# Lists for the routed experts' tiles: one list of forty made at the end, or a first list of nine made early and the rest later

## The chip, the core and the metric

The kernel runs on one core of one Trainium2 chip. The engines are PE (TensorE, matrix products), DVE (VectorE), ACT (ScalarE), POOL (GpSimd) and SP (SyncE, which here only issues DMAs). They run side by side and meet at semaphores. The metric is the device time of one execution in microseconds, lower is better.

## The reference, cut to what matters

A small vision network of five parts works on 8 x 257 = 2056 tokens of 256 values: a state-space tokenizer, an attention, a layer of routed experts, a second attention with a feed-forward part, and a quantised feed-forward. The change touches the routed experts alone:

```python
xf = x.reshape(-1, C)                       # 2056 x 256, normalised rows
gate_logits = xf @ Wr                       # 8 experts
w, idx = jax.lax.top_k(gate_logits, TOP_K)  # TOP_K = 2
w = jax.nn.softmax(w, axis=-1)
comb = jnp.sum(w[:, :, None] * jax.nn.one_hot(idx, NUM_EXPERTS, dtype=w.dtype), axis=1)
h = jnp.einsum('nc,ech->neh', xf, W1)       # hidden width 384
g = jnp.einsum('nc,ech->neh', xf, W3)
y = jnp.einsum('neh,ehc->nec', jax.nn.silu(h) * g, W2)
out = jnp.einsum('nec,ne->nc', y, comb)
```

## The kernel before, in words

The kernel is one program of stages, each a block in which every engine has its own instruction stream; a stage begins when all engines are through the one before. `routed_experts` (from L1022) is the third of six. It computes only what the routing asks for: each token's row goes to its two experts, and the experts' rows are worked off in tiles of 128.

**Tokens and groups.** The tokens lie in SBUF as 17 tiles of 128 rows (`TILES`; the last, `CLS`, has 8 rows: the class tokens). They are routed in five groups (`GROUPS`, L1083): tiles 0 to 1, 2 to 3, 4 to 7, 8 to 11, 12 to 16. For each group, PE turns the normalised rows and multiplies them with the gate's matrix (L1405, L1416); DVE's `choose(g)` (L1218 to L1239) finds the two largest of eight logits and writes `sel`, a one for each chosen expert; PE's `ranks(g)` (L1425, L1429) counts with triangular and all-one matrices how many rows of each expert stand before each token, in one PSUM bank (`RB` = 3); DVE's `place_rows(g)` (L1243 to L1260) turns the count into two row numbers for each token in the HBM buffer `x_rows`, where each expert has a region of 17 tiles (`REGION`), and raises `placed`. Behind the reading of the counts it raises `rank_read`.

**Scatters.** POOL (L1156 to L1163) writes the rows into `x_rows` with indirect DMAs, two for each token tile, 34 in all, one after the other, each group behind its `placed`. Those of the first eight token tiles (`FIRST_ROWS`) count on the semaphore `scattered_first`, the others on `scattered`.

**Expert tiles.** There is room for 40 (`NT`) expert tiles of 128 rows. The first nine (`FULL`) are taken from regions that the first eight token tiles alone fill to whole tiles of 128 (8 x 128 x 2 rows over 8 experts give at least nine of them). `full_tiles()` (L1264 to L1275), behind the third group's placing, counts them: `cum` is the running sum by expert, cut at nine, and `used` how many of the nine each expert gives. The other 31 take what is left, expert by expert.

**The list.** Behind `place_rows(4)`, DVE makes one list for all 40 tiles (L1296 to L1330): from `used` and the remaining number of tiles it forms running sums (`ends`) over 16 parts, compares each tile number with each of them (`past`, 40 x 16 = 640 elements in each partition), and derives from that the expert of each tile (`owner_i`) and the row in `x_rows` where it starts (`row_i`), by sums over the 16 parts. L1330 raises `owned`. Behind the list (L1332 to L1353) DVE computes where in the packed output each token's two rows will be (`packed`, `pos_i`) and (L1355 to L1370) the two weights of each token (`share`); both are read in the next stage. ACT's exponential for the weights (L1176) waits for the differences of L1297.

**The order of the stage's second half.** SP waits for `owned` (L1103). `load(t)` (L1106 to L1114) reads the row number of tile t from `row_i` into a register (L1107), for t = 0 waits for `scattered_first`, for t = 9 for `scattered`, from t = 4 on for a free buffer of four, and loads 128 rows of `x_rows` into `xin`. The first four loads come at once, then one in each turn of a loop that also stores results. PE waits for `owned` (L1441); then `turn_rows(t)` (L1443) transposes the loaded tile into banks 0 and 1, `up` (L1452) makes the two products with the expert's W1 and W3 (banks 2 to 5), `turn_hidden` (L1459) transposes the hidden rows, `down` (L1468) multiplies with W2. In the loop from L1479 PE's order for tile t is: transpose rows of t + 1, `up` 0 of t, transpose hidden of t - 1, `up` 1 of t, `down` of t - 1. ACT copies transposed rows (L1182), computes SiLU (L1196) and copies results (L1189). DVE's loop (L1386 to L1390) has only `turned(t - 1)` (copy of transposed hidden rows, L1383) and `hidden(t)` (SiLU times second product, L1377).

`s(...)` issues an instruction that counts on the engine's own semaphore; `s.wait()` waits for all that were issued before. Dependent steps are so separated by it.

## Time and profile before

| | |
|---|---|
| Median of three runs | 1336.87 us (1335.01 to 1336.89) |
| The profiled execution | 1331.12 us, its span 1329.4 us |
| Mean granted clock of PE in it | 0.865 of full speed |
| Busy over the span | PE 83%, DVE 59%, POOL 35%, ACT 29% |
| The routed experts' stage | from about 250 to 480 us |

The profile is one execution, recorded by the hardware; the durations below all come from it. Times in microseconds count from the start of its span. A timeline row gives start, length, engine, line and operation, what is written and read, and in brackets how long the engine had been idle and what ended that. Granted clock 1.00 is 2.4 GHz, 0.50 is 1.2 GHz.

### The profile page before, as it was taken

How to read it: one execution, taken by the hardware profiler on the slowest of the kernel's cores; microseconds unless marked ns; L12 is line 12 of the kernel's file. 1: busy time of each engine (PE TensorE's matmuls, PEld its weight loads, DVE VectorE, ACT ScalarE, POOL GpSimd, SP SyncE). 2: the span in 40 equal slices, each digit the busy share in tenths (PEclk: the TensorE clock that was granted, in tenths of full speed). 3: DMA queues.
4: the chain of work that ended last, by engine and by line, in shares of the span. 5: the costliest groups of instructions: out<-in, count | busy, mean ns of one | idle time of the engine just before them, and what ended most of it. 6: DMA issues, size and time to landing. Idle time of an engine off the chain costs nothing. (4 is left out here: it accounts for less than half of the span.)

```text
span 1329.4 us, 22071 instructions
## 1 busy us (share of the span) xinstructions
PE 1105.6 (83%) x6752; PEld 792.8 (60%) x6752; DVE 780.3 (59%) x1860; ACT 385.7 (29%) x951; POOL 467.3 (35%) x579
## 2 busy tenths in 40 slices
PE   0267898859999945799999999999889999689898
PEld 0166776556777722556656566565548998455555
DVE  8965666562222233667575575755733776588884
ACT  0242333102222211233343333432304443222221
POOL 4962000271000035122232222220115776376665
PEclk9978999659999977578696886967778999799999
DMA  9908000222111116155152461523214000000000
GB/s 318 307 1 285 1 0 0 72 103 77 61 60 60 60 33 115 48 94 110 48 109 73 79 114 39 109 76 48 83 35 137 0 0 0 1 9 8 16 16 17
DMA packets 66431, 93.81 MB, mean 71 GB/s; under 512 B 9152, under 2 KB 58760, under 8 KB 65200
## 3 DMA queue, kind: packets, MB, share of 16 engines
q1 hardware_dynamic: 63152, 84.42, 24.3%
q0 software_dynamic: 3200, 8.43, 2.0%
q8 instruction: 38, 0.62, 0.2%
q14 instruction: 41, 0.34, 0.1%
HBM read 52.23 MB, written 40.33 MB: 70 GB/s over the span
## 5 line engine op out<-in xcount | busy, mean ns | idle before, releaser
L2200 DVE TENSOR_REDUCE fa_nm<-fa_ps 128x2 f32<-128x514 f32 x128 | 83.0, 690 | 84.2 <-PE fa_ps L2442 83.5
L1455 PE MATMUL ex_ps<-we_raw,ex_xT 128*128 x320 | 117.5, 490 | 0.0
L1993 ACT ACTIVATE fa_eT<-fa_ps 128x512 f32<-128x512 f32 x128 | 73.6, 590 | 71.1 <-PE fa_ps L2495 69.7
L3243 PE MATMUL qf_ps<-qf_wg,qf_xT 128*128 128x352 f32 x272 | 90.0, 480 | 2.1 <-ACT qf_xT L3084 1.4
L2442 PE MATMUL fa_ps<-fa_ks,fa_qs 64*128 64x258 f32 x256 | 73.5, 419 | 21.6 <-DMA fa_ks<-fa_qk_rows 16.9
L451 PE MATMUL tk_ps<-tk_u,tk_qb 64*32 64x64 f32 x1024 | 24.8, 274 | 69.6 <-POOLq L318 56.7
L1383 DVE COPY ex_hT<-ex_ps 128x384 f32<-128x384 f32 x40 | 22.3, 559 | 100.1 <-PE ex_ps L1464 100.1
L2442 PEld LDWEIGHTS fa_ps<-fa_ks,fa_qs 64*128 64x128 f32 x256 | 52.7, 268 | 47.2 <-issue 30.7
L2495 PE MATMUL fa_ps<-fa_qs,fa_ks 66*128 66x256 f32 x256 | 71.1, 372 | 7.0 <-ACT fa_eT L1993 7.0
L3243 PEld LDWEIGHTS qf_ps<-qf_wg,qf_xT 128*128 128x128 f32 x272 | 50.7, 195 | 37.3 <-issue 6.8
L1455 PEld LDWEIGHTS ex_ps<-we_raw,ex_xT 128*128 128x128 f32 x320 | 55.4, 193 | 22.1 <-issue 1.1
L2874 PE MATMUL ff_ps<-ff_xT,wg_f 128*128 128x128 f32 x544 | 65.9, 282 | 3.2 <-ACT ff_xT L2773 3.2
L2874 PEld LDWEIGHTS ff_ps<-ff_xT,wg_f 128*128 128x128 f32 x544 | 65.7, 198 | 4.3 <-issue 3.5
L3231 PE MATMUL qf_ps<-qf_wd,qf_hT 128*128 128x256 f32 x204 | 53.2, 404 | 17.5 <-DVEq L3152 12.0
L2888 PE MATMUL ff_ps<-wg_f,ff_hid 128*128 128x256 f32 x272 | 63.1, 386 | 2.8 <-DVEq L2814 2.8
L451 PEld LDWEIGHTS tk_ps<-tk_u,tk_qb 64*32 64x32 f32 x1024 | 22.9, 146 | 71.3 <-issue 71.3
L2495 PEld LDWEIGHTS fa_ps<-fa_qs,fa_ks 66*128 66x128 f32 x256 | 43.9, 209 | 34.3 <-issue 20.0
L1765 POOL DMA_INDIRECT fa_xn<-y_rows,pos_i x2 | 1.8, 878 | 175.9 <-POOLq L1098 175.6
L1473 PE MATMUL ex_ps<-we_raw,ex_hT 128*128 x240 | 58.4, 379 | 0.7 <-DVE ex_hT L1383 0.7
L2888 PEld LDWEIGHTS ff_ps<-wg_f,ff_hid 128*128 128x128 f32 x272 | 51.4, 194 | 9.7 <-issue 3.2
L3231 PEld LDWEIGHTS qf_ps<-qf_wd,qf_hT 128*128 128x128 f32 x204 | 36.9, 194 | 31.2 <-ACT qf_hT L3095 21.3
L2780 ACT ACTIVATE ff_hid<-ff_ps,wg_c 128x128 f32<-128x128 f32 x136 | 37.0, 383 | 61.7 <-PE ff_ps L2874 61.7
(487 smaller groups left out, 2487.8 us busy)
## 6 DMA issues: line engine op xcount, KB each, us to landing
x_rows<-tk_zero SPq DMA_DIRECT2D x8, 2176.0 KB, 17.5
we_raw<-in_L_ffn_W SPq DMA_DIRECT2D x24, 384.0 KB, 7.3
fa_qs<-fa_qk_rows SPq DMA_DIRECT2D x16, 514.0 KB, 8.7
fa_ks<-fa_qk_rows SPq DMA_DIRECT2D x32, 257.0 KB, 10.7
ex_xin<-x_rows SPq DMA_DIRECT2D x40, 128.0 KB, 2.0
y_rows<-ex_y SPq DMA_DIRECT2D x40, 128.0 KB, 1.7
fa_rsb<-fa_rs_rows SPq DMA_DIRECT2D x32, 132.0 KB, 2.8
fa_qk_rows<-fa_qhl SPq DMA_DIRECT2D x32, 128.5 KB
```

The source lines that it names most:

```text
L451: last = nc.tensor.matmul(ps[outs, p, i * n:(i + 1) * n], QB[rows, p, r, j * HB // 2 + i, :], U[rows, p, r, j * HB // 2 + i, :], start=(r ...
L1455: last = mm(ps[:, bank + t % 2, 0:HD], xT[:, t % 2, k, :], raw[:, ds(e, 1), m, k * HD:(k + 1) * HD], start=(k == 0), stop=(k == KC - 1))
L1473: last = mm(ps[:, YB, 0:SEQ], hT[:, t % 2, j, :], raw[:, ds(e, 1), 2, j * SEQ:(j + 1) * SEQ], start=(j == 0), stop=(j == NJ - 1))
L1993: cp(eT[:, j % 8, :], ps[:, ST + j % 2, :], ACT.Exp).then_inc(z["e_ready"], 1)
L2200: nc.vector.tensor_reduce(nm[:, :, j], ps[:, b:b + 2, 0:TOK], AX.X, ALU.max, negate=True).then_inc(z["max_done"], 1)
L2442: last = mm(ps[:, b + t, 0:WID], qs[0:ROWS, p, head(j, 1 + t * P, P)], ks[0:ROWS, p, head(j, 0, WID)], start=True, stop=True)
L2495: last = mm(ps[:, ST + j % 2, c * SEQ:(c + 1) * SEQ], ks[0:ROWS + 2, p, head(j, 1 + c * P, P)], qs[0:ROWS + 2, p, head(j, 1, SEQ)], start= ...
L2780: nc.scalar.activation(hid[:, p, f, :], ps[:, HB + 2 * p + f // 4, (f % 4) * P:(f % 4 + 1) * P], ACT.Relu, bias=w["c1"][:, f:f + 1]).then_ ...
L2874: last = mm(ps[:, HB + 2 * p + f // 4, (f % 4) * P:(f % 4 + 1) * P], w["f1"][:, k, f * P:(f + 1) * P], xT[:, p, k, :], start=(k == 0), sto ...
L2888: last = mm(ps[:, YB + p, 0:SEQ], hid[:, p, f, :], w["f2"][:, f, :], start=(f == 0), stop=(f == NF - 1))
L3231: last = mm(ps[:, YB, 0:SEQ], hT[0:n, c, :], wd[0:n, c, :], start=(c == 0), stop=(c == NH6 - 1))
L3243: last = mm(ps[:, GB + 2 * g + a, 0:HALF], xT[:, k, :], wg[:, g, k, a * HALF:(a + 1) * HALF], start=(k == 0), stop=(k == KC - 1))
```

## The change

DVE's one list becomes two. `first_list()` makes owners and rows of tiles 0 to 8 and runs behind `choose(3)`, ahead of `place_rows(3)`; it uses `cum` directly (8 parts for 9 tiles: 72 elements). The list of the other 31 tiles (8 parts, 248 elements) is cut in three: `other_parts()` stands behind `place_rows(4)`, `other_owners()` behind the hidden product of tile 0, `other_rows()` behind that of tile 1. `packing()`, `positions()`, `weights()` and the two `shares()` stand behind those of tiles 2 to 6. The differences for the weights move ahead of `place_rows(4)`. `owned` is now raised twice: SP and PE wait for the first at their start, and for the second at tile 9 (`FULL`). PE gets a wait for the fifth `rank_read` ahead of the first `turn_rows`, since the counts' bank and the logits' banks are used again. Three memsets and one wait of POOL at the stage's start go. The numbers that come out are the same.

```diff
@@ experts, SP @@
             def load(t):
+                if t == FULL:
+                    sp.wait_ge(z["owned"], 2)
                 rows[t] = nc.sync.value_load(row_i[0:1, t:t + 1], min_val=0, max_val=(ROW_TILES - 1) * P)
                 if t == 0:
                     sp.wait_ge(z["scattered_first"], 16 * 2 * FIRST_ROWS)
@@ experts, POOL @@
-            s(g.memset(next_owner[:, :], 1.0))
             s(g.memset(cum[:, 0:1], 0.0))
-            s(g.memset(off[:, 2 * NE:2 * NE + 1], float(ROW_TILES - 1)))
-            s.wait()
-            s(g.memset(next_owner[:, NE - 1:NE], float(1 - NE)))
-            s(g.memset(next_owner[:, 2 * NE - 1:2 * NE], 0.0))
+            s(g.memset(off[:, :, NE:NE + 1], float(ROW_TILES - 1)))
             s.wait()
@@ experts, DVE, place_rows @@
                 if hi == FIRST_ROWS:
                     s(ts(full_i[:, :], rank[:, hi, :], 0.0, None, ALU.add))
+                if hi == TILES:
+                    s(ts(cnti[:, :], rank[:, hi, :], float(P - 1), None, ALU.add))
                 s.wait()
                 dve.sem_inc(z["rank_read"], 1)
@@ experts, DVE @@
+            FIRST, REST = slice(0, FULL), slice(FULL, NT)
+
+            def first_list():
+                s(tt(past[:, FIRST, :], bc(nth[:, FIRST], 2, NE), bc(cum[:, 1:NE + 1], 1, FULL), ALU.is_ge))
+                s(tt(off[:, 0, 0:NE], region[:, :], cum[:, 0:NE], ALU.subtract))
+                s.wait()
+                s(nc.vector.tensor_reduce(owner[:, FIRST], past[:, FIRST, :], AX.X, ALU.add))
+                s(tt(step[:, 0, :], off[:, 0, 1:NE + 1], off[:, 0, 0:NE], ALU.subtract))
+                s.wait()
+                s(tt(behind[:, FIRST, :], past[:, FIRST, :], bc(step[:, 0, :], 1, FULL), ALU.mult))
+                s(ts(owner_i[:, FIRST], owner[:, FIRST], float(NE - 1), None, ALU.min))
+                s.wait()
+                s(nc.vector.tensor_reduce(begin[:, FIRST], behind[:, FIRST, :], AX.X, ALU.add))
+                s.wait()
+                s(tt(begin[:, FIRST], nth[:, FIRST], begin[:, FIRST], ALU.add))
+                s.wait()
+                s(ts(row_i[:, FIRST], begin[:, FIRST], float(ROW_TILES - 1), float(P), ALU.min, ALU.mult))
+                s.wait()
+                dve.sem_inc(z["owned"], 1)
+
+            def other_parts():
+                s(ts(cnti[:, :], cnti[:, :], 7, None, ALU.logical_shift_right))
+                s.wait()
+                s(nc.vector.tensor_copy(cnt[:, :], cnti[:, :]))
+                s.wait()
+                s(tt(parts[:, :], cnt[:, :], used[:, :], ALU.subtract))
+                s.wait()
+                s(nc.vector.tensor_tensor_scan(ends[:, :], ones[:, 0:NE], parts[:, :], 0.0, ALU.mult, ALU.add))
+                s.wait()
+                s(tt(past[:, REST, :], bc(nth[:, 0:NT - FULL], 2, NE), bc(ends[:, :], 1, NT - FULL), ALU.is_ge))
+                s(tt(start[:, :], ends[:, :], parts[:, :], ALU.subtract))
+                s.wait()
+                s(tt(ahead[:, :], used[:, :], start[:, :], ALU.subtract))
+                s.wait()
+
+            def other_owners():
+                s(nc.vector.tensor_reduce(owner[:, REST], past[:, REST, :], AX.X, ALU.add))
+                s(tt(off[:, 1, 0:NE], region[:, :], ahead[:, :], ALU.add))
+                s.wait()
+                s(ts(owner_i[:, REST], owner[:, REST], float(NE - 1), None, ALU.min))
+                s(tt(step[:, 1, :], off[:, 1, 1:NE + 1], off[:, 1, 0:NE], ALU.subtract))
+                s.wait()
+                s(tt(behind[:, REST, :], past[:, REST, :], bc(step[:, 1, :], 1, NT - FULL), ALU.mult))
+                s.wait()
+
+            def other_rows():
+                s(nc.vector.tensor_reduce(begin[:, REST], behind[:, REST, :], AX.X, ALU.add))
+                s.wait()
+                s(stt(begin[:, REST], nth[:, 0:NT - FULL], off[:, 1, 0:1], begin[:, REST], ALU.add, ALU.add))
+                s.wait()
+                s(ts(row_i[:, REST], begin[:, REST], float(ROW_TILES - 1), float(P), ALU.min, ALU.mult))
+                s.wait()
+                dve.sem_inc(z["owned"], 1)
...
             choose(3)
+            first_list()
             place_rows(3)
             choose(4)
+            differences()
             place_rows(4)
-
-            s(ts(cnti[:, :], rank[:, TILES, :], float(P - 1), None, ALU.add))
-            s(tt(wt[:, :, :], lg[:, :, 0:NE], top[:, :, 0:1].broadcast_to([P, TILES, NE]), ALU.subtract))
...
-            s(tt(past[:, :, :], bc(nth[:, :], 2, 2 * NE), bc(ends[:, :, :].rearrange("p a e -> p (a e)"), 1, NT), ALU.is_ge))
...
-            s(tt(behind[:, :, :], past[:, :, :], bc(next_owner[:, :], 1, NT), ALU.mult))
...
-            dve.sem_inc(z["owned"], 1)
...
+            other_parts()
...
                 hidden(t)
+                if t == 0:
+                    other_owners()
+                elif t == 1:
+                    other_rows()
+                elif t == 2:
+                    packing()
+                elif t == 3:
+                    positions()
+                elif t == 4:
+                    weights()
+                elif t == 5:
+                    shares(0)
+                elif t == 6:
+                    shares(1)
             turned(NT - 1)
@@ experts, PE @@
             owners = [None] * NT
+            pe.wait_ge(z["rank_read"], len(GROUPS))
             turn_rows(0)
             for t in range(NT):
+                if t == FULL:
+                    pe.wait_ge(z["owned"], 2)
                 owners[t] = nc.tensor.value_load(owner_i[0:1, t:t + 1], min_val=0, max_val=NE - 1)
```

`packing()`, `positions()`, `weights()` and `shares(a)` hold the old L1332 to L1346, L1348 to L1353, L1355 to L1363 and one turn of L1364 to L1370, with `jump` formed from `ahead` and `cum` in one operation.

## Rows read from the trace of the kernel before

**Rows 1.** Windows of core 0, busy us of each engine in two stretches
```profile
core 0: us, PE busy (x) PEld busy (x) DVE busy (x) ACT busy (x) POOL busy (x), PEclk, DMA share, GB/s
256.00:294.00 38.00, 27.31 (x129) 26.91 (x127) 22.87 (x132) 4.08 (x8) 24.53 (x24) 0.50 0.29 108
294.00:300.00 6.00, 1.11 (x4) 0.75 (x5) 5.30 (x24) 1.43 (x2) 4.48 (x6) 0.50 0.46 151
```

**Rows 2.** Timeline of PE, 284 to 304 us: start, length, idle before and releaser
```profile
284.02 2.28 PE L1429 MATMUL ex_ps<-ex_sel,ex_ones 128*128 128x40 f32 x10
297.85 0.66 PE L1448 MATMUL ex_ps<-ident,ex_xin 128*128 128x128 f32 x2 [11.55 <-DMA ex_xin<-x_rows]
299.55 0.69 PE L1448 MATMUL ex_ps<-ident,ex_xin 128*128 128x128 f32 x2 [1.03 <-DMA ex_xin<-x_rows]
300.03 3.90 PE L1455 MATMUL ex_ps<-we_raw,ex_xT 128*128 x8
```

**Rows 3.** Waits of SP's own queue, 255 to 330 us
```profile
SPq L1107 <- DVEq L1330: 37.2, 1, 37.2
```

**Rows 4.** Timeline of SP's queue, first loads and that of tile 9
```profile
295.67 5.51 SPq L1114 DMA_DIRECT2D ex_xin<-x_rows  x5
...
327.64 0.33 SPq L1114 DMA_DIRECT2D ex_xin<-x_rows  x1
```

**Rows 5.** Instructions that read ex_row_i: shortest, median, longest ns; first start
```profile
L1107 SPq TENSOR_LOAD <-ex_row_i x40: 262/269/531, 294.7 to 459.6; - x40
```

**Rows 6.** Timeline of DVE, 275 to 297 us
```profile
275.56 0.19 DVE L1237 TENSOR_TENSOR ex_sel<-ex_lr,ex_valid 128x32 f32<-128x32 f32 x1
278.27 0.19 DVE L1246 TENSOR_TENSOR ex_place<-ex_ps,ex_base 128x32 f32<-128x32 f32 x1 [2.52 <-PE ex_ps L1429]
...
286.34 0.20 DVE L1246 TENSOR_TENSOR ex_place<-ex_ps,ex_base 128x40 f32<-128x40 f32 x1 [2.88 <-PE ex_ps L1429]
286.69 0.20 DVE L1251 TENSOR_TENSOR ex_place<-ex_place,ex_sel 128x40 f32<-128x40 f32 x1
...
289.31 0.82 DVE L1310 TENSOR_TENSOR ex_past<-ex_nth,ex_ends 128x640 f32<-128x640 f32 x1
...
291.26 0.81 DVE L1317 TENSOR_REDUCE ex_owner<-ex_behind 128x40 f32<-128x640 f32 x1
...
294.36 0.23 DVE L1328 TENSOR_SCALAR ex_row_i<-ex_begin 128x40 int32<-128x40 f32 x1
294.74 0.17 DVE L1332 SCALAR_TENSOR_TENSOR ex_delta<-ex_start,ex_base 128x8 f32<-128x8 f32 x1 [0.15 <-DVE ex_row_i L1328]
...
296.91 0.30 DVE L1348 TENSOR_REDUCE ex_pos<-ex_packed 128x17 f32<-128x136 f32 x1
```

**Rows 7.** Timeline of POOL: the sixteenth scatter, a stretched one, the last
```profile
281.73 0.96 POOL L1160 DMA_INDIRECT x_rows<-ex_xn,ex_into  x1 [0.30 <-issue]
...
289.36 1.59 POOL L1160 DMA_INDIRECT x_rows<-ex_xn,ex_into  x1 [0.30 <-issue]
...
305.79 0.85 POOL L1160 DMA_INDIRECT x_rows<-ex_xn,ex_into  x1 [0.31 <-issue]
```

**Rows 8.** Line L1160 (scatters): time from issue to landing
```profile
DMA to landing us min/median/max: 2.0/2.4/3.2
```

**Rows 9.** Timeline of DVE in the first expert tiles
```profile
304.02 0.55 DVE L1377 TENSOR_TENSOR ex_hid<-ex_sl,ex_ps 128x384 f32<-128x384 f32 x1 [3.02 <-PE ex_ps L1455]
305.80 0.56 DVE L1383 COPY ex_hT<-ex_ps 128x384 f32<-128x384 f32 x1 [1.22 <-PE ex_ps L1464]
...
310.23 0.56 DVE L1383 COPY ex_hT<-ex_ps 128x384 f32<-128x384 f32 x1 [2.58 <-PE ex_ps L1464]
```

**Rows 10.** Timeline of PE in the first expert tiles
```profile
306.89 1.46 PE L1473 MATMUL ex_ps<-we_raw,ex_hT 128*128 x6
...
311.32 1.46 PE L1473 MATMUL ex_ps<-we_raw,ex_hT 128*128 x6
```

**Rows 11.** Windows of core 0, the microsecond with the clock's rise (columns as above)
```profile
302.00:303.00 1.00, 1.00 (x4) 0.67 (x3) 0.00 (x0) 0.33 (x1) 0.93 (x1) 0.83 0.73 250
```

133 lines of the change are left out of this document (55 added, 78 removed).

## The prediction

> **What bounds the kernel now.** I read the windows first, by stretch of the experts' stage. From 256 to 294 us PE works on gate logits and ranks for 27.3 of 38 us; from 294 to 300 it is busy for 1.11 of 6 us while DVE is busy for 5.30 [rows 1]. From the first expert product on, the PE timeline has no idle time until the stage's last tile. So the stage is bound by PE as soon as the first tile runs, and the stretch before that by something else. The page's chain of waits does not reach this stretch, so I follow the hand-over with the timelines. On PE, the last rank product ends at 286.30 and the first transposition of gathered rows starts at 297.85: 11.55 us idle, put down to the load of ex_xin [rows 2]. On SP's own queue, the read of the first row number waited 37.2 us for DVE's semaphore of L1330; it starts at 294.7, and the first load at 295.67 [rows 3 to 5]. On DVE, the last placing starts at 286.34, and the list of the 40 tiles' owners and rows ends with L1328, which starts at 294.36 [rows 6]. So the first load is late because of one chain of small operations on DVE; its data, the first eight tiles' scattered rows, had landed long before (next part). Whatever brings that load forward brings the whole PE-bound stage forward.
>
> **The first list, moved.** It has six dependent steps, four of them on 9 x 8 = 72 elements (three have a second, independent operation beside). The 128x40 operation takes 0.20 us and the 128x136 one 0.30 [rows 6], so 72 elements take about 0.23; with 0.03 to 0.04 between dependent ones and some 0.1 for each second operation the list is about 1.8 us. It starts where L1237 of the fourth group ends, 275.75, and ends at about 277.6. The next DVE instruction waits for PE until 278.27, an idle time of 2.52 us [rows 6]: that is the cover, and the cost is nothing. If it took 1 us more, only the fourth group's scatters would wait, and POOL reaches those behind the sixteenth, at 283.0 (281.73 and 1.26 more [rows 7]).
>
> **What holds the first load next.** SP reads the first row number at 277.7 and then waits for the 16 scatters of the first eight tiles. POOL issues them one after the other, 1.26 us apart; the sixteenth starts at 281.73 and lands 2.0 to 3.2 us later, median 2.4 [rows 7, 8]: 284.13, bounds 283.73 and 284.93. The row number is read by then. Behind its read, of 0.53 us at most, the old load started at 295.67, 0.44 after 295.23 [rows 4, 5]: that is the upper bound from release to load, nothing the lower one, and I take the middle, 0.2 us. So the first load starts at 284.33 instead of 295.67: **11.34 us earlier**, between 11.94 and 10.30.
>
> **What else could hold PE.** PE's new wait is for the fifth reading of the ranks. L1251 starts at 286.69, behind that reading [rows 6]; the change puts one more 128x8 operation ahead of it, 0.08 us: 286.8. Behind this wait stands all of PE's work for tile 0, but the load lands at 284.33 + 2.18 = 286.5 (297.85 less 295.67), so the first transposition starts at 286.8 and ends at 287.5. The second tile's load is what counts before the first product: it came 3.88 us after the first load's start (299.55 less 295.67), and the product 4.36 after it (300.03) [rows 2, 4]. In the new kernel that is 288.2 and 288.7. Both are past 287.5, so the wait for the ranks costs nothing; it would count only if it ended past 287.5. The load of old competed with a busier DMA, so up to 0.5 us more could be gained; I leave it out. **Term: 11.3 us.**
>
> **The rest of the list** (other_parts): seven operations of 8 elements and one of 31 x 8 = 248. From 136 elements in 0.30 and 640 in 0.81 [rows 6], 248 take 0.42. About 1.8 us from 287.8 to 289.6; DVE's first product comes at 304.02 - 11.3 = 292.7. Hidden; the cover has 3 us to spare. The old list had five operations of 640 elements, 4.1 us in all; the new one has four of 248 and four of 72.
>
> **The parts dealt out among the tiles.** Each stands behind hidden(t) and ahead of turned(t). In the first gap DVE idles 1.22 us, later 2.58 us [rows 9]. turned(0) ends at 306.36 and PE's next product that needs it starts at 306.89; for tile 1 these are 310.79 and 311.32 [rows 9, 10]: so 0.53 us of slack more. The pieces: other_owners two of 248 and small ones, 0.54 + 0.30 + 0.46 = 1.3 us against 1.22 + 0.53; other_rows 1.0; packing, from L1332 at 294.74 to L1348 at 296.91, 2.17 [rows 6]; positions 1.0, weights 1.3 and each share 1.0, by their steps of 136 elements at 0.30 and 0.03 between (positions two, side by side, and two short ones; weights four; a share three); these against 2.58 + 0.53 = 3.11. All fit. If the cover were gone, their 8.8 us would come onto the path. The tightest are the first, with 0.45 us to spare, and packing, with 0.94.
>
> **Waits of tile 9.** The old kernel issues the load of tile 9 (counted from 0) at 327.64 [rows 4]; the new one at 316.3. The last scatter starts at 305.79 [rows 7] and lands at 308.2, or 309.0 at the most; the second part of the list is ready behind hidden(1), 296.3 + 1.0. Both new and old waits find their semaphores up, with 7 us of margin. Differences before the last placing: 0.3 us in an idle stretch of 2.88 [rows 6]; memsets taken from POOL at the start of the stage: nothing waits for them. Nothing behind this stage is changed, so it should all move forward by the same amount.
>
> **Sum.** 11.3 us off the profiled execution's 1331.12 us gives 1319.8. The median of the runs shown is 1336.87, which is 5.75 above that execution; the same 11.3 us there gives **1325.6 us**.
>
> **A rule against the change.** While POOL scattered, DVE's operations kept their times: the 640-element L1310, with a scatter beside it, took 0.82 us and L1317 0.81. But that scatter, begun 0.05 us after L1310, took 1.59 us instead of 0.96 [rows 6, 7]. So a DVE operation with two inputs delays a scatter by about its own rest; 72-element ones ahead of the sixteenth scatter cost at most 0.1 each, 0.2 in all, within the bounds. The Trainium skill, "SBUF — State Buffer", in its part on ports and contention, says that VectorE and GpSimd share a port pair as an exclusive lock: whichever starts first holds it for its whole instruction, also against a VectorE operation with two SBUF inputs. By that rule the DVE pieces could be the blocked side too, which no row here shows.
>
> **The rivals.**
> (a) *DVE's pieces are held by scatters.* Scatters run until 306, so the pieces behind tiles 0, 1 and 2 (292.7 to 303) share the time with them. If each piece were held once for a whole scatter of 0.96: other_owners 2.3 against 1.75, packing 3.1 against 3.1; held twice, packing is 1 us late. That is 0.5 to 3 us for three pieces: gain 8.3 to 10.8, 1328.6 to 1326.1 us. Against it: the even DVE times above.
> (b) *PE's clock, the side that is slower.* The granted clock was 0.50 up to 300 and 0.83 in the mean of 302 to 303 [rows 1, 11]: with 0.50 before the rise and 1.00 behind it, PE went from 1.2 to 2.4 GHz at about 302.3. It had worked without gaps since 299.55. Eight products took 3.90 us over it [rows 2], some 0.64 us apart before and 0.33 behind it, so a tile at 1.2 GHz costs 4.4 us more than the 4.43 us that it takes (311.32 less 306.89 [rows 10]). The new start has the same order of work and the same gaps, so the rise should come at the same distance, within a microsecond either way, worth 0.5. But if small gaps from a late DVE piece kept the clock down for two tiles, 8.8 us are given back: 1334.4, no change. From 2.6 tiles on the kernel is slower; with three it gains 11.3 - 13.3 = -2.0, with four -6.4: 1338.9 to 1343.3 us. The page "TensorE: Matmul & The Clock Gate" of the Trainium skill says, in its part on the clock gate, that the activity window runs freely and the number of slow matmuls varies from run to run; by that the half microsecond is luck. Against (b): the work up to 294 kept PE at 0.50 though it was nearly always busy, so no earned clock is lost by the change.
> (c) *The hole only moves.* If the first load went on waiting for something of DVE's last group, or tile 9 stalled on the scatters, what is gained at 297 is lost at 316. The code excludes the first (the semaphore is raised behind L1237's group, before the last placing); the second needs scatters 7 us late, where the stretched one of old was 0.63 late (1.59 less 0.96). Full loss gives 1336.9, no change. That the change doesn't do what it says is this rival too.
> (d) *More than the forecast.* The second load lands 0.5 us sooner and the clock rises up to 2 us sooner: gain 12.8, 1324.1 us, or 1323 with the landing at its minimum.
>
> **How the numbers follow.** Forecast 0.80; (a) 0.07; (b) 0.04, half of it no change and half slower; (c) 0.02; (d) 0.07. The range: gain 12.8 plus 0.5 for the landing, and about 1.5 us of scatter between medians (the three runs shown lie within 1.9 us) gives the low end, 1322; the high end takes in the bounds (10.3), a late clock (0.5), most of (a) and the same scatter: a gain of 5.9, 1331. A change of 0.2% is 2.7 us, about what a measurement of this kernel can tell from none. Faster 0.94, no change 0.04, slower 0.02.
>
> **What would show it.** First ex_xin load at 284.3 (wrong if past 285.5); first transposition at 286.8, released by the ranks rather than by the load; first product at 288.7; DVE's small operations between its tile operations with PE's products without gaps from there; PE's tile rhythm 4.43 us; load of tile 9 at about 316; the stage's last product ends at 467.6 instead of 478.9. Wrong would be: gaps on PE behind DVE ex_hT in tiles 0 to 6, a granted clock of 0.50 beyond 292, or PE waiting at tile 9.

## The result and the profile after

| | before | after |
|---|---|---|
| median of 20 executions each (us) | 1338.69 (1333.48 to 1347.76) | 1333.24 (1326.50 to 1338.30) |
| ratio after to before, 95% interval | | 0.9949 (0.9935 to 0.9963) |
| profiled execution (us) | 1331.12 | 1337.93 |
| its span (us) | 1329.4 | 1336.2 |

The change makes the kernel faster by 5.45 us, where 11.3 us were forecast, and the time, 1333.24 us, is above the range of 1322 to 1331. Put beside each other, the two profiled executions say the opposite, 6.8 us slower. The execution of before that was profiled was shorter than each of the 20 executions behind the median of before. That turns out to be part of the explanation, so each distance below is given with the execution it is from. By the ratio's interval the gain lies between 5.0 and 8.7 us. Of the 6.8 us between the two profiled executions, 3.0 stand at the stage's last product (219.28 us behind the first scatter against 216.24) and 3.8 come in the stages behind it.

The windows of the changed kernel (columns as in [rows 1]):

```profile
core 0: us, PE busy (x) PEld busy (x) DVE busy (x) ACT busy (x) POOL busy (x), PEclk, DMA share, GB/s
256.00:300.00 44.00, 29.53 (x135) 28.32 (x134) 20.09 (x131) 5.67 (x10) 24.29 (x25) 0.50 0.31 112
300.00:314.00 14.00, 10.98 (x39) 6.54 (x38) 4.48 (x15) 2.35 (x8) 8.46 (x9) 0.92 0.19 77
314.00:345.00 31.00, 30.89 (x132) 21.63 (x133) 13.10 (x38) 8.34 (x23) 0.00 (x0) 1.00 0.21 65
```

From 256 to 300 us PE is busy for 29.5 us, hardly more than in the two rows of [rows 1] together (28.4), although the load of gathered rows was to come 11 us earlier. From 314 us on PE is full at clock 1.00; from 300 to 314 it misses 3 us.

The timeline of PE, changed kernel (start, length, line, idle before it and releaser; as in [rows 2, 10]):

```profile
291.55 0.65 PE L1469 MATMUL ex_ps<-ex_sel,ex_before 128*128 128x40 f32 x2 [8.92 <-DVEq L1238]
292.00 2.28 PE L1473 MATMUL ex_ps<-ex_sel,ex_ones 128*128 128x40 f32 x10
297.70 0.66 PE L1492 MATMUL ex_ps<-ident,ex_xin 128*128 128x128 f32 x2 [3.42 <-issue]
...
299.05 4.37 PE L1499 MATMUL ex_ps<-we_raw,ex_xT 128*128 x8
...
309.53 1.46 PE L1499 MATMUL ex_ps<-we_raw,ex_xT 128*128 x4
314.11 1.56 PE L1517 MATMUL ex_ps<-we_raw,ex_hT 128*128 x6 [3.13 <-DVE ex_hT L1413]
...
318.64 1.46 PE L1517 MATMUL ex_ps<-we_raw,ex_hT 128*128 x6
...
323.06 1.46 PE L1517 MATMUL ex_ps<-we_raw,ex_hT 128*128 x6
```

The first transposition of gathered rows (L1492) starts at 297.70, almost where it was (297.85 [rows 2]) and not at 286.8. Two holes stand ahead of it: 8.92 us ahead of the fifth group's rank products (L1469), and 3.42 us ahead of the transposition, with no DMA as the releaser. A third, of 3.13 us, follows at tile 1 (314.11). From 318.64 on the rhythm is 4.42 us a tile.

SP's queue and the first of the reads of the row numbers, changed kernel ([rows 4, 5] before; the second fence is the view of line L1110):

```profile
285.79 13.08 SPq L1117 DMA_DIRECT2D ex_xin<-x_rows  x5
```

```profile
L1110 SPq TENSOR_LOAD <-ex_row_i x40: 3/269/700, 279.1 to 462.7; - x40
```

The row number was read at 279.1 and the first load went out at 285.79, 9.88 us earlier than at 295.67 [rows 4]. So the part of the change that its name speaks of did happen. But the five loads of this group took 13.08 us in place of 5.51. The fifth waits for a free buffer; the first four have no wait between them in the code, and they start at 285.79, 288.61, 295.68 and 297.23, over 11.44 us where the kernel before needs 3.88 (295.67 to 299.55).

The timeline of DVE, changed kernel ([rows 6, 9] before):

```profile
277.33 0.23 DVE L1279 TENSOR_TENSOR ex_past<-ex_nth,ex_cum 128x72 f32<-128x72 f32 x1
...
278.84 0.23 DVE L1292 TENSOR_SCALAR ex_row_i<-ex_begin 128x9 int32<-128x9 f32 x1
...
286.55 0.20 DVE L1220 COPY ex_lg<-ex_ps 128x40 f32<-128x40 f32 x1 [5.60 <-remote]
...
288.67 0.20 DVE L1232 TENSOR_TENSOR ex_lr<-ex_lr,ex_lg 128x40 f32<-128x40 f32 x1 [0.37 <-DVE ex_lr L1229]
290.07 0.20 DVE L1236 TENSOR_TENSOR ex_sel<-ex_lr,ex_valid 128x40 f32<-128x40 f32 x1 [1.20 <-DVE ex_lr L1232]
...
297.27 0.20 DVE L1245 TENSOR_TENSOR ex_place<-ex_ps,ex_base 128x40 f32<-128x40 f32 x1 [5.38 <-remote]
...
299.60 0.42 DVE L1305 TENSOR_TENSOR ex_past<-ex_nth,ex_ends 128x248 f32<-128x248 f32 x1
...
303.52 0.55 DVE L1407 TENSOR_TENSOR ex_hid<-ex_sl,ex_ps 128x384 f32<-128x384 f32 x1 [3.23 <-PE ex_ps L1499]
...
309.47 0.18 DVE L1326 TENSOR_SCALAR ex_row_i<-ex_begin 128x31 int32<-128x31 f32 x1
313.41 0.56 DVE L1413 COPY ex_hT<-ex_ps 128x384 f32<-128x384 f32 x1 [3.76 <-remote]
```

The last placing (L1245) starts at 297.27; before it started at 286.34 [rows 6]. PE had ended its rank products at 294.28 (292.00 + 2.28), so DVE saw them 3 us late. The choice of the fifth group (L1220, 286.55) was 3.9 us late: PE's gate logits had ended at 282.64. Even between two operations of DVE itself, L1232 and L1236, stand 1.20 us where the same pair of the third group, at 268.15 and 268.38, has 0.04. At tile 1, PE's transposition L1508 ended at 309.69 and DVE took it up at 313.41. The word "remote" is the profile's for a release that it can't place at any instruction of this moment. ACT shows the same at the same time, its first store of ex_y waiting 7.52 us:

```profile
313.26 0.38 ACT L1188 ACTIVATE ex_y<-ex_ps 128x256 f32<-128x256 f32 x1 [7.52 <-remote]
```

What runs beside all this is POOL with its scatters:

```profile
261.12 1.25 POOL L1159 DMA_INDIRECT x_rows<-ex_xn,ex_into  x1 [7.58 <-DVEq L1261]
...
270.27 0.98 POOL L1159 DMA_INDIRECT x_rows<-ex_xn,ex_into  x1 [0.30 <-issue]
274.36 0.95 POOL L1159 DMA_INDIRECT x_rows<-ex_xn,ex_into  x1 [3.10 <-DVEq L1261]
...
293.29 0.96 POOL L1159 DMA_INDIRECT x_rows<-ex_xn,ex_into  x1 [0.30 <-issue]
298.96 0.96 POOL L1159 DMA_INDIRECT x_rows<-ex_xn,ex_into  x1 [4.70 <-DVEq L1261]
...
310.26 0.85 POOL L1159 DMA_INDIRECT x_rows<-ex_xn,ex_into  x1 [0.31 <-issue]
```

They come in three trains, that is rows of scatters with no more than 0.31 us of idle time between two, one scatter each 1.26 us (1.31 in the first): 8 of them up to 271, 16 from 274.36 to 294.25 and 10 from 298.96 to 311.1. The late hand-overs lie in the trains and end 2 to 3 us behind them: 297.27 behind 294.25, 313.3 behind 311.1.

### The profile page after: what moved, and what is told of

The parts are those of the page before. It is cut to its first block and busy times, and to the rows that moved or that the text cites. A ratio compares the mean times of both kernels' runs of the same rounds, so it can differ in the third digit from the quotient of the medians.

```text
span 1336.2 us, 22077 instructions
## 1 busy us (share of the span) xinstructions
PE 1107.7 (83%) x6752; PEld 794.3 (59%) x6752; DVE 777.3 (58%) x1867; ACT 385.0 (29%) x951; POOL 465.6 (35%) x576
## 5 line engine op out<-in xcount | busy, mean ns | idle before, releaser
L2489 PEld LDWEIGHTS fa_ps<-fa_ks,fa_qs 64*128 64x128 f32 x256 | 53.5, 273 | 45.4 <-issue 29.5
L1413 DVE COPY ex_hT<-ex_ps 128x384 f32<-128x384 f32 x40 | 22.3, 558 | 95.3 <-PE ex_ps L1508 91.5
L1517 PEld LDWEIGHTS ex_ps<-we_raw,ex_hT 128*128 128x128 f32 x240 | 45.3, 190 | 19.1 <-issue 5.4
```

The lines of the kernel that those rows point to most:

```text
L1517: last = mm(ps[:, YB, 0:SEQ], hT[:, t % 2, j, :], raw[:, ds(e, 1), 2, j * SEQ:(j + 1) * SEQ], start=(j == 0), stop=(j == NJ - 1))
L2489: last = mm(ps[:, b + t, 0:WID], qs[0:ROWS, p, head(j, 1 + t * P, P)], ks[0:ROWS, p, head(j, 0, WID)], start=True, stop=True)
```

## The experiments

All times below are from profiles where not said otherwise. So that executions can be laid over each other, events are counted from the start of the first scatter of the same execution. "Placing" is the last placing on DVE, "load" the first load of gathered rows, "first" the first transposition of them on PE and "end" the last expert product; each is a start. `scatter_late` is not in the table, since its first scatter comes only behind its last placing.

| run | placing | load | first | end |
|---|---|---|---|---|
| before, the profile shown ahead | 25.20 | 34.53 | 36.71 | 216.24 |
| before_a | 35.79 | 45.04 | 47.24 | 228.17 |
| before_b | 35.74 | 45.00 | 47.26 | 226.72 |
| before_2 | 35.74 | 45.00 | 47.26 | 226.69 |
| after | 36.15 | 24.67 | 36.58 | 219.28 |
| again | 36.18 | 24.73 | 36.62 | 219.31 |
| change_2 | 35.81 | 24.58 | 36.24 | 218.81 |
| first_only | 36.17 | 24.70 | 36.61 | 222.29 |
| deal_only | 36.05 | 40.51 | 42.59 | 223.58 |
| held | 36.16 | 37.79 | 39.83 | 225.78 |
| paced | 36.25 | 25.64 | 36.68 | 219.66 |
| paced_before | 36.18 | 45.49 | 47.65 | 228.45 |
| half | 25.14 | 17.96 | 25.57 | 204.37 |
| half_before | 25.19 | 34.44 | 36.66 | 217.02 |
| break_once | 29.77 | 24.71 | 30.19 | 226.98 |
| breaks | 29.79 | 24.70 | 30.22 | 209.33 |
| breaks_2 | 29.57 | 24.58 | 30.01 | 210.01 |
| breaks_before | 25.19 | 34.43 | 36.59 | 217.80 |
| breaks_before_2 | 27.44 | 36.68 | 38.82 | 219.98 |

**The change again, and taken apart.** `again` is the changed kernel unaltered. `first_only` keeps the early list and has all the other pieces in one block; `deal_only` keeps the dealing and makes the first list late; `held` lets the early load wait for the last placing.

```diff
 # first_only
             other_parts()
+            other_owners()
+            other_rows()
+            packing()
+            positions()
+            weights()
+            shares(0)
+            shares(1)
...
-                if t == 0:
-                    other_owners()
...
 # deal_only
             choose(3)
-            first_list()
             place_rows(3)
...
             place_rows(4)
+            first_list()
             other_parts()
 # held
                 if t == 0:
+                    sp.wait_ge(z["placed"], len(GROUPS))
                     sp.wait_ge(z["scattered_first"], 16 * 2 * FIRST_ROWS)
```

> The changed kernel once more, to see whether its delays stand at the same places. In its first profile the first load started at 285.79 us, as forecast but for 1.45 us, and then engines waited 1 to 5 us for signals that had long been raised (DVE 5.60 and 5.38 us before L1220 and L1245, ACT 7.52 and DVE 3.76 us at tile 1). Theory A, the early loads bring this about: the same delays come again between 283 and 315 us, first product past 296 us, ratio to the kernel before 0.995. Theory B, a disturbance that falls anywhere and hit this profile: the delays are elsewhere or smaller, first product at 288.7 to 291, stage about 11 us ahead of the kernel before.

> The first list moved as in the change, but nothing dealt out: all the rest stands in one block behind the last placing (10.6 us from 287.8 to 298.4). If nothing disturbs, the first product of DVE is 5.5 us late and the gain is 5.8 us, ratio 0.9957. Theory A (delays belong to loads and scatters side by side): the delays stand here too, in the same stretch, and the gain is near nothing or the same as the full change's. Theory C (delays come from the pieces among the tiles): no delays, gain 5.8 us.

> Pieces dealt out as in the change, but the first list made behind the last placing, so that the first load starts at about 290.7 us instead of 295.7. Undisturbed gain 5.0 us, ratio 0.9963. Theory A: loads beside scatters again for 10 us, so delays as in the change. Theory C (delays come from the pieces): delays at tiles 0 to 2 as in the change (3.8 us at tile 1). Theory B: none or anywhere.

> The changed kernel, but SP's first load also waits for the last placing (287.8 us): first load 288.0, 3.7 us later than it could be, first product at 292.4. Undisturbed the gain is 7.6 us, ratio 0.9943. Theory A in its narrow form (loads during the last group's choice and ranks slow DVE's and PE's signals): no delays before 288 us and the kernel is as fast as the change or faster. Theory D (a long wait on a register-loaded load or on the scatters' semaphore by SP slows the signals of others): delays between 279 and 288 as before.

Measured, on one chip with 29 executions of before at 1340.83 us: again 1330.34 us, ratio 0.9927 (0.9902 to 0.9952); first_only 1333.83, 0.9953 (0.9929 to 0.9976); deal_only 1335.06, 0.9952 (0.9933 to 0.9971); held 1332.67, 0.9946 (0.9923 to 0.9969). All four are faster than before, and the intervals of the four ratios overlap, so the totals hardly tell them apart. The rows do. `again` repeats the profile of after to a tenth: the placing at 36.2 and the start of PE at 36.6 are no accident of one execution. `held` puts the load 13.1 us later and loses only 3.2 at the first transposition, so in the changed kernel PE is not waiting for the load: its wait for the fifth reading of the ranks is the one that ends last. In `held` and `deal_only` the first load goes out only behind the last placing, and the placing is as late (36.16 and 36.05), so the early loads don't bring the delay about. At the last product `first_only` is 3.0 us later than `again`, `deal_only` 4.3 and `held` 6.5. In `held`, 3.2 of these stand at the first transposition; the rest is mostly the clock: behind its hole of 3.14 us at tile 1 the granted clock is 0.50 (in the mean of 313 to 318 us), where `again` keeps 1.00 behind one of 2.99. What the block costs stands in the timeline of PE, first_only:

```profile
308.26 0.90 PE L1501 MATMUL ex_ps<-ident,ex_hid 128*128 128x128 f32 x3 [4.64 <-issue]
```

DVE is busy with the block and PE waits 4.64 us for the first hidden rows. Of the 8.8 us that the prediction set for the pieces without cover, 4.64 show as this hole. Behind it the granted clock is 0.50 up to 311 us and 0.82 in the mean of 311 to 312; some 3 us of work at half the clock cost 1.6 more. Against that, first_only has none of the hole of some 3 us that the changed kernel has at tile 1 (2.99 in `again`). The sum, 3.2, is near the 3.0 measured at the last product.

**Before, profiled twice more, and the scatters moved.** Is the late placing made by the change, and is it made by the scatters? `before_a` and `before_b` are the kernel before, unaltered. `scatter_late` is the changed kernel with all scatters behind the last placing.

```diff
             clear_spent(pool, mem)
 
+            pool.wait_ge(z["placed"], len(GROUPS))
             for t in range(TILES):
```

> The kernel before, profiled again. All four traces of changed kernels have the same delays between PE's and DVE's hand-overs from 270 to 297 us (DVE's L1245 of the third group 1.5 us late, the last choice 4 to 6 us late, the last placing 9.4 to 11 us late), also the one whose work up to 286 us is that of the kernel before. Theory E, the first profile of the kernel before was an unusually quiet execution: then the same delays stand here, its last placing at 296 to 297.5 us, its first load at 305 to 307, its span at 1338 to 1343. Theory F, the changed kernels bring the delays: last placing at 286.3 again, span near 1330.

> The same again, as a second draw. Theory E: last placing at 296 to 297.5 us; theory F: 286.3.

> The changed kernel, but POOL begins its scatters only behind the last placing, so that none runs beside the choosing and ranking. If the scatters (or their landings) delay the hand-overs between PE and DVE, then DVE's last placing starts at about 286.5 us without the scatters; if the delays have another source, it stands at 296 to 297.5 as before. The first load then waits for 16 scatters from about 288 (297.5) us, 20 us, so the kernel is slower: first product near 313 us (quiet) or 323, total 1337 to 1345 either way.

Measured, one execution each: 1344.63, 1339.40 and 1360.94 us, beside one of before at 1340.72. The timelines of DVE, PE and POOL of before_a:

```profile
296.86 0.20 DVE L1246 TENSOR_TENSOR ex_place<-ex_ps,ex_base 128x40 f32<-128x40 f32 x1 [11.19 <-remote]
```

```profile
286.23 2.28 PE L1429 MATMUL ex_ps<-ex_sel,ex_ones 128*128 128x40 f32 x10
308.31 0.66 PE L1448 MATMUL ex_ps<-ident,ex_xin 128*128 128x128 f32 x2 [19.80 <-DMA ex_xin<-x_rows]
```

```profile
293.23 0.96 POOL L1160 DMA_INDIRECT x_rows<-ex_xn,ex_into  x1 [0.31 <-issue]
298.47 1.02 POOL L1160 DMA_INDIRECT x_rows<-ex_xn,ex_into  x1 [4.28 <-DVEq L1260]
```

The kernel before has the same fault. Its PE ended the rank products at 288.51, and DVE took them up at 296.86: 8.35 us late, 2.7 us behind the end of the train at 294.19. In the profile that stands ahead of the prediction DVE idles 2.88 us there [rows 6]; here it idles 11.19. So PE starts its tiles at 47.24 behind the first scatter, not at 36.71. Both executions, and later a third (before_2), agree within 0.05 us on that. Of the four profiles of this kernel, the one on which the prediction rests is the exception.

The timeline of DVE in scatter_late, and the last scatter in that of POOL:

```profile
284.87 0.20 DVE L1246 TENSOR_TENSOR ex_place<-ex_ps,ex_base 128x40 f32<-128x40 f32 x1 [2.43 <-PE ex_ps L1474]
...
334.31 0.56 DVE L1414 COPY ex_hT<-ex_ps 128x384 f32<-128x384 f32 x1 [13.74 <-remote]
```

```profile
328.64 0.85 POOL L1160 DMA_INDIRECT x_rows<-ex_xn,ex_into  x1 [0.31 <-issue]
```

With no scatter beside them the ranks run as in the quiet profile: the last placing starts at 284.87 after 2.43 us of idle time. Then one train of 34 scatters runs from 286.59 to 329.5, and the late hand-overs go with it. DVE takes up the transposed hidden rows of tile 0 at 334.31, 13.2 us behind their end on PE at 321.11, and the release is again "remote". The delays follow the scatters, not the place in the code and not the change. They also cost more here than was expected: 1360.94 us against a forecast of 1337 to 1345.

**How many scatters are open.** One explanation was the number of scatters under way at a time. `paced` and `paced_before` let POOL wait, before the scatters of token tile t, until those of tile t - 2 have landed (semaphores split by parity), in the changed kernel and in the old one.

```diff
             for t in range(TILES):
                 n = rows_of(t)
+                if t >= 2:
+                    u = t - 2
+                    name, lo = ("scattered_first%d", 0) if u < FIRST_ROWS else ("scattered%d", FIRST_ROWS)
+                    pool.wait_ge(z[name % (u % 2)], 16 * 2 * ((u - lo) // 2 + 1))
```

`half` and `half_before` issue only one of the two scatters of each token tile, in either kernel. Half of the expert rows then keep what was there, so their results are not the reference's; the rest of the work is the same.

```diff
-                    sp.wait_ge(z["scattered_first"], 16 * 2 * FIRST_ROWS)
+                    sp.wait_ge(z["scattered_first"], 16 * FIRST_ROWS)
...
-                for a in range(2):
+                for a in range(1):
```

> The changed kernel, with POOL holding back the scatters of a token tile until those of the tile two before have landed (so at most four under way; undisturbed a scatter lands 2.4 us after its start and the next two take 2.5, so the hold costs nothing). Theory G1, the hand-overs are late because completions of scatters pile up: few under way, no pile, last placing near 286.5 us, first product at 288.7, ratio to the kernel before 0.985. Theory G2, it is the rate of one scatter every 1.26 us for more than 10 us that does it, not how many are open: delays as in the change, scatters either unchanged or later, ratio 0.994 or worse.

> The same holding back on the kernel before. G1: last placing at 286.3, first load at 295.7 as in its first, quiet profile, ratio 0.994 to the kernel before; the paced change is then faster than this by the 11.3 us of the forecast. G2: last placing at 295 to 297 us, ratio 1.000 or worse.

> The changed kernel with only one of a token's two scatters (half of the expert rows stay at what they were, the rest of the work is the same), so the train is 17 long instead of 34, at the same rate. If the delay grows with the length of the unbroken train, the eight scatters behind the third placing (10 us) delay DVE's hand-overs by 0 to 1.5 us, last placing at 286.5 to 288.5 and first load near 281 to 284, no delay at tile 1. If any scatter beside the hand-over delays it, the delays stay at 4 us and more.

> The kernel before with only one of a token's two scatters, to be set against the changed kernel with the same cut, where no hand-over was late (last placing 283.79 us, first transposition 284.22, stage ahead by 23 us). If the change is worth what the forecast said once no hand-over is late, this one has its first transposition at 295.3 us and takes 10.5 to 12 us more than the changed one cut in the same way: 1327 to 1329 us. If dealing out or the early list costs something by itself, the difference is under 8 us.

Measured: paced 1333.70 us, 0.9954 (0.9934 to 0.9973); paced_before 1341.78, 1.0004 (0.9988 to 1.0020), both beside a before of 1340.17; half 1316.74 in one execution, half_before 1325.18 in one. The pacing does nothing: placing at 36.25 and 36.18, as without it. At most four scatters can be open in it, and the distance between them stayed at 1.26 us. That excludes more than four open scatters as the cause, and no more: a scatter lands 2.0 to 3.2 us after its start in the profile of before [rows 8], so at 1.26 us apart hardly more than three are open anyway, and the added wait never held POOL (0.31 us idle at most inside the trains). Leaving half of them out removes the late hand-overs, in one execution of each kernel, on chips where before ran at 1340. The timelines of DVE, PE and POOL of half:

```profile
283.79 0.20 DVE L1245 TENSOR_TENSOR ex_place<-ex_ps,ex_base 128x40 f32<-128x40 f32 x1 [2.43 <-PE ex_ps L1473]
```

```profile
281.03 0.65 PE L1469 MATMUL ex_ps<-ex_sel,ex_before 128*128 128x40 f32 x2 [2.53 <-DVEq L1238]
281.48 2.28 PE L1473 MATMUL ex_ps<-ex_sel,ex_ones 128*128 128x40 f32 x10
284.22 0.66 PE L1492 MATMUL ex_ps<-ident,ex_xin 128*128 128x128 f32 x2 [0.47 <-issue]
```

```profile
274.00 0.96 POOL L1159 DMA_INDIRECT x_rows<-ex_xn,ex_into  x1 [0.30 <-issue]
277.42 0.96 POOL L1159 DMA_INDIRECT x_rows<-ex_xn,ex_into  x1 [2.46 <-DVEq L1261]
```

The placing is back at 25.14 with its 2.43 us of idle time, and the first transposition starts 0.47 us behind the rank products, as the prediction had it. (The first load goes out at 276.61, earlier than expected, since it waits for eight scatters only.) POOL's scatters now come in trains of four at most (five at the end), with 1.8 us or more between them. This pair also gives the price of the change without late hand-overs: 36.66 less 25.57 is **11.1 us** at the first transposition (11.3 forecast, from an old start at 36.71), 12.65 us at the last product and 8.4 us in the time of the two executions, which were not made on the same chip; `half_before` was expected to take 10.5 to 12 us more. The last product gains 1.56 us more than the first transposition, and most of it is the clock: from the second transposition to the rise of the granted clock `half` needs 2.7 us (0.60 in the mean of 287 to 288) and `half_before` 4.9 (0.71 in that of 303 to 304), and 2.2 us longer at half the clock cost 1.1. In the other direction, the stages behind the last product took 6.2 us longer in `half`.

**Breaking the train.** If it is the unbroken train that matters, the same 34 scatters with breaks should do. `break_once` holds the last 18 of them until the last placing is done. `breaks` adds five more breaks, each by a wait of POOL for PE's down projection of an early tile.

```diff
+    BREAKS = {11: 1, 12: 2, 13: 3, 14: 4, 15: 5}
...
                 pool.wait_ge(z["placed"], 1 + sum(t >= hi for _, hi in GROUPS))
+                if t == FIRST_ROWS:
+                    pool.wait_ge(z["placed"], len(GROUPS))
+                if t in BREAKS:
+                    pool.wait_ge(z["y_ps"], BREAKS[t])
```

(`break_once` has the first of the two conditions alone.)

> The changed kernel, but POOL stops behind its sixteenth scatter until the last placing is done, so that the last choice and ranks have no scatters beside them; the other 18 then run in one train beside the first expert tiles. Theory G2 (an unbroken train of more than some 10 us delays the hand-overs): last placing near 287 us, first product near 290, but then tiles 1 to 4 stall for up to 10 us until the train ends at about 312 us; total between 1325 and 1336. If only the choice and ranks suffer: 1321.

> As the last, and the 18 later scatters are also broken up: six at once, then the next token tiles behind the finished products of expert tiles 0 to 4 (two scatters each, four at the end). Theory G2: neither the ranks nor the tiles stall, last scatter lands at about 322 us, just in time for tile 9; first product at 289 to 290, no gap on PE behind it, total 1320 to 1323, ratio 0.985 to 0.988. If the breaks are too short to matter: 1328 to 1334 as the change.

Measured, beside a before of 1339.76 us: break_once 1339.86 us, 0.9993 (0.9976 to 1.0010); breaks **1322.95 us, 0.9866 (0.9839 to 0.9892)**. The timelines of PE in break_once, and of PE and POOL in breaks:

```profile
317.26 2.92 PE L1519 MATMUL ex_ps<-we_raw,ex_hT 128*128 x6 [14.31 <-DVE ex_hT L1415]
```

```profile
288.20 0.65 PE L1474 MATMUL ex_ps<-ex_sel,ex_before 128*128 128x40 f32 x2 [5.49 <-DVEq L1243]
...
291.39 0.66 PE L1497 MATMUL ex_ps<-ident,ex_xin 128*128 128x128 f32 x2 [0.47 <-issue]
```

```profile
283.27 0.96 POOL L1164 DMA_INDIRECT x_rows<-ex_xn,ex_into  x1 [0.30 <-issue]
293.16 0.96 POOL L1164 DMA_INDIRECT x_rows<-ex_xn,ex_into  x1 [8.93 <-DVEq L1266]
...
299.48 0.96 POOL L1164 DMA_INDIRECT x_rows<-ex_xn,ex_into  x1 [0.30 <-issue]
302.55 0.96 POOL L1164 DMA_INDIRECT x_rows<-ex_xn,ex_into  x1 [2.11 <-PE ex_ps L1522]
```

In break_once the placing comes at 29.77 instead of 36.2 and PE starts 6.4 us earlier, but all of it is lost again, and 7.7 us more at the last product (the median, 1339.86, lies above the 1325 to 1336 expected): the remaining 18 scatters form one train, from 290.91 to 313.2, and PE stands still for 14.31 us at tile 1, until 4 us behind it. With breaks, the last 18 come as six, four times two and four, with 1.8 to 2.2 us of idle time on POOL between them; PE has no such hole, and the last product comes 10 us earlier than in the changed kernel (209.33 against 219.31). What is left is in the first 16 scatters: behind the train of eight, 274.42 to 284.2, PE still waits 5.49 us for DVE's choice (2.53 in half).

**The breaks without the change, and all side by side.** `breaks_before` and `breaks_before_2` put the same breaks into the kernel before; `breaks_2`, `change_2` and `before_2` repeat breaks, after and before.

> The kernel before with the same breaks among the scatters as in the last kernel, so that in neither a hand-over is much delayed; the two differ by the change alone. If the forecast's sum holds for such a kernel, the first transposition stands about 38 us behind the first scatter (25.2 to 27.1 for the last placing, 9.3 for the list, 2.2 for the load), 9 to 11.3 us behind that of the changed kernel with breaks, the ratio to the kernel before is 0.993 to 0.996 and 0.992 for changed against unchanged. If the breaks alone gave the 17 us, it is at 0.987 to 0.989 too.

> The changed kernel with breaks among the scatters. Where hand-overs are late without breaks: first transposition 30.2 us behind the first scatter, no stall behind it, ratio 0.986 to 0.988. Where they are not late (a quiet chip or time): as the changed kernel alone within 1 us.

> The kernel before with breaks. Where hand-overs are late without them: 4 to 7 us faster than the kernel before (ratio 0.995 to 0.997), and 8 to 11 us slower than the changed kernel with breaks. In a quiet time: ratio 1.000.

> The changed kernel once more, side by side with the next three on one chip, since in the last run the kernel before itself took 1329.8 us instead of 1340: there the delays may be missing on a chip or for a time. Forecast of the sum: first transposition 10 to 11.3 us ahead of the kernel before where no hand-over is late (then ratio 0.992, and 11.3 us), 10.7 where both are late (47.3 less 36.6 us behind the first scatter), of which tile 1's stall takes 3 back: ratio 0.993 to 0.995.

> The kernel before, for its profile next to those three. Late hand-overs: last placing 35.7 us behind the first scatter and span near 1338. Quiet: 25.2 us and span near 1329.

Measured, the first alone: breaks_before 1329.72 us beside a before of 1329.77 on the same chip, 1.0005 (0.9985 to 1.0025). The profile of breaks_before has no late hand-over (placing at 25.19), and before itself, of which no profile was taken on that chip, was 10 us below its other medians; so most likely that chip, or that hour, had none at all, and the ratio says that breaks neither help nor hurt a kernel whose hand-overs are on time. It says nothing on the cause. The changed kernel did not run there: what the change is worth where nothing is late is shown by the pair half and half_before alone.

The other four ran together on another chip, with 23 executions of before at 1339.81 us:

| | median us | ratio to before (95%) | first | end |
|---|---|---|---|---|
| before_2 (one execution) | 1341.69 | | 47.26 | 226.69 |
| change_2 | 1331.57 | 0.9952 (0.9928 to 0.9977) | 36.24 | 218.81 |
| breaks_before_2 | 1333.75 | 0.9961 (0.9938 to 0.9984) | 38.82 | 219.98 |
| breaks_2 | 1325.36 | 0.9900 (0.9869 to 0.9931) | 30.01 | 210.01 |

PE's first transposition, in breaks_2 and in breaks_before_2:

```profile
290.76 0.66 PE L1497 MATMUL ex_ps<-ident,ex_xin 128*128 128x128 f32 x2 [0.47 <-issue]
```

```profile
298.37 0.66 PE L1453 MATMUL ex_ps<-ident,ex_xin 128*128 128x128 f32 x2 [11.42 <-DMA ex_xin<-x_rows]
```

Change and breaks add up, though breaks_2 at 0.990 stays short of the 0.986 to 0.988 expected. Either alone takes 6 to 8 us off the 1339.81, both take 14.5. On the broken trains the change is worth 8.8 us at the first transposition (38.82 less 30.01), 10.0 at the last product and 8.4 in the medians; on the unbroken ones 11.0, 7.9 and 8.2.

**What else goes with the delays.** The profiles show three more things that bear on the cause. First, each scatter raises its semaphore 16 times when its rows have landed, and a trace has a record of each raise: 544 for 34 scatters. In the two profiles with 34 scatters and no late hand-over (before, breaks_before) all 544 are there. In the sixteen others there are only 106 to 266, and in half and half_before, which have no late hand-over, 126 and 177 of 272. The profile gives a time to landing only where none is missing, as its lists of issues show, in before and in before_a:

```profile
x_rows<-ex_xn,ex_into POOLq DMA_INDIRECT x34, 2.4
```

```profile
x_rows<-ex_xn,ex_into POOLq DMA_INDIRECT x34
```

Second, it is not only the hand-overs that are slow. SP's MOVE before each load only sets a register and waits for no other engine; here are its shortest, median and longest time in ns, in before and in after:

```profile
L1114 SPq MOVE ex_xin<-x_rows x40: 29/29/38, 295.6 to 460.3; - x40
```

```profile
L1117 SPq MOVE ex_xin<-x_rows x40: 29/29/701, 285.7 to 463.3; - x40
```

Third, the engine that waits is not the late part: the record of PE's raise for the last placing stands at 297.24 in after and at 296.83 in before_a, and DVE starts 0.03 us behind it. PE's products had ended at 294.28 and 288.51 by the profile, which models the ends of products.

So there is a rival that no run tests: the recording itself. Either the train of scatters slows the engines and the recording suffers with them, or writing so many records is what slows the engines. The executions that are listed one by one, also behind the medians, all have a recorded span and clock; none is known to show the kernel unrecorded. Nor does any run set the scatters evenly further apart, so the length of a train and the rate of scatters are not told apart: half and breaks change both.

## Why the prediction was wrong

**The first list and the load: right.** first_list ran from 277.33 to 279.07, 1.74 us for a forecast of 1.8, and the placing behind it came 0.12 us later than in before_a, where it stood at 279.58. The sixteenth scatter started at 283.18, 1.45 us later than forecast, because the third placing was late already (272.70, behind 2.28 us of idle time; 271.25 behind 0.81 in the profile of before); the load followed it by 2.61 us, forecast 2.60.

**"What else could hold PE": wrong, and this is the step that failed.** It put the fifth reading of the ranks at 286.8 and said that the wait would count only past 287.5. The reading ended at about 297.6, and the transposition started at 297.70. If it landed as fast as before, in 2.18 us, the first load's rows had been there for 9.7 us; by `held`, 13.1 us of its lead are worth only 3.2 us at this point. The term was worked out from rows of one execution whose hand-overs were on time, and the change is what makes PE's start hang on a hand-over beside a train of scatters. That the scatters bring the delay is shown by moving them (scatter_late, placing after 2.43 us of idle time), by halving them and by breaks; by what means they do is open. "What holds the first load next" missed a smaller part of the same: the loads behind the first were late too, the third at 295.68, which stays hidden because PE starts only at 297.70.

**The base: wrong in the same way, and partly making up for it.** The 11.3 us were taken off a median, as if its executions looked like the profiled one. The sign that they don't was in the prediction's own sum: the profiled execution lay 5.75 us below the median, and below all three runs shown. Where late hand-overs occur, the old chain carries the late placing too (35.8 in place of 25.2) and puts its list behind it: it starts PE at 47.26. From there the gain at the first transposition is 47.26 less 36.6, **10.7 us**, near the forecast by another road than the one written down: that it is so near is luck.

**"The parts dealt out": right in size, wrong in what PE does next.** The pieces took 1.41 us (other_owners), 2.13 (packing), 0.91 (positions), 1.25 (weights) and 0.96 (a share), against 1.3, 2.17, 1.0, 1.3 and 1.0. PE waited for none of them. But it lost 3.13 us at tile 1 to a hand-over that was late beside the last train of scatters. The old kernel started its tiles when most of that train was over: it has no such hole. So the gain shrinks from 10.7 us at the first transposition to between 7.4 and 8.9 at the last product (226.7 and 228.2 against 219.3). The 1.5 us between the two ends of before are the clock: from the second transposition to the rise before_a needs 5.9 us (0.61 in the mean of 315 to 316), before_b 3.0.

**From the stage to the whole.** The stage's 7.4 to 8.9 us compare with 8.2 us in the medians of change_2 and its before, and with 5.45 in the first measurement, whose interval ends at 8.7 us (0.0065 of 1338.69). How much of the smaller figure is the share of executions without late hand-overs, and how much the later stages is not settled: from the last product to the end of the span, the changed kernel needs 855.8 us in after and 849.2 in again, the kernel before 851.5 to 853.7.

**The rivals.** (a), pieces held by scatters: no; the 248-element operations took 0.40 to 0.42 us with a scatter beside them. The Trainium skill, "SBUF — State Buffer", on ports and contention, gives VectorE and GpSimd an exclusive lock on a shared port pair. The rows of after show no such block: L1305, with two inputs, starts at 299.60 inside the scatter of 298.96 to 299.92 and takes its 0.42 us. The most that a piece lost is 0.25 us (L1315, 0.43 against 0.18 in change_2); and a lock held for one scatter, 0.96 us, is too short for delays of 3 to 8 us. (b), the clock: not in after; the granted clock of 0.50 up to 300 and 0.92 in the mean from 300 to 314 puts the rise from 1.2 to 2.4 GHz at about 302.2, some 3.6 us behind the start of work without gaps (298.58), for 2.8 before. But the distance is not as fixed as (b) took it: it is 2.7 to 6.0 us over the profiles here, and holes of 3.14 us (held) and 4.64 us (first_only) did bring the clock back to 0.50. What the prediction says against (b), that PE was nearly always busy up to 294, is not in its rows: 27.3 of 38 us. (c), the hole only moves: the nearest, though not for its reason. The load no longer waited for the list and tile 9 found its semaphores up, but of the 11.3 us the 3 at tile 1 did come back as a hole of another kind.

## What to carry to other kernels

Before a wait is moved, ask which hand-over becomes the last one, and look at it in several profiles of the kernel as it is: one execution, here shorter than all the twenty of its median, can hide a 10 us delay that the three other profiles of the kernel have. A profiled time below all the runs beside it is a warning. Where POOL issues a long row of indirect scatters, treat hand-overs between the other engines beside it and shortly behind it as uncertain, and try breaking the row up with waits that cost nothing, every two to six scatters. It paid here as measured; whether it would without the recording is not shown. A change whose gain stays away can still be right: with the train broken, this one is part of the fastest version, with ratios of 0.990 and 0.987 to the kernel before.

## What the runs showed of the hardware

- Beside an unbroken train of indirect scatters, one each 1.26 us, releases between engines came late in 16 of 20 profiles: by 3.0, 3.7 and 3.9 us in after, 8.35 in before_a and 13.2 in scatter_late, all on DVE, and through DVE in PE (14.31 us idle in break_once). ACT idled 7.52 us at the same time in after. SP started its first four loads over 11.44 us in after and 19.34 in scatter_late instead of 3.88, and single register steps of it took 701 ns instead of 38. The delays cleared 2 to 5 us behind the train's last scatter. Operations of DVE kept their durations or lost up to 0.25 us: L1413 took 0.56 us throughout.
- A train of 8 cost about 3 us in a hand-over behind it (5.49 less 2.53), and less in breaks_before_2, whose placing stands at 27.44 for 25.20; trains of 10 to 18 cost 3 to 14 us, trains of 2 to 6 with some 2 us between them nothing. Holding the number of open scatters at four, without lengthening the distance between issues, changed nothing.
- It doesn't happen in every execution: the first profile of before and that of breaks_before, on a chip where the median of before was 1329.77 us, were free of it, and these two are the only ones with all 544 records of landings. The waiting engine reacts at once (0.03 us). Whether the scatters or the recording beside them slow the engines, and what makes a chip or an hour free of it, stays open.
- With the granted clock at 0.50 before it, PE's clock rose from 1.2 to 2.4 GHz 2.7 us (half) to 6.0 (scatter_late) behind the second transposition, where PE's dense work began. It fell back to 1.2 GHz at holes of 3.14 us (held), 4.64 (first_only) and 14.31 (break_once), and stayed at 2.4 GHz at those of 3.13 (after) and 2.99 (again).
